# Order and grain of the first steps of a ternary feed-forward stage: rows in four groups, the second matrix's size read later, its ternary form made in three parts

## The reference

```python
def absmax_quant(x):
    gamma = jnp.max(jnp.abs(x), axis=-1, keepdims=True)
    x_hat = jnp.clip(x * Q_B / gamma, -Q_B + EPS, Q_B - EPS)
    return x_hat * gamma / Q_B
def ternarize_weights(w):
    gamma = jnp.mean(jnp.abs(w))
    return jnp.sign(jnp.round(w / (gamma + EPS))) * gamma
def bitlinear(x, w):
    xn = layer_norm(x)
    x_hat = absmax_quant(xn)              # value of the straight-through form
    w_hat = ternarize_weights(w)
    return jnp.einsum('bsd,od->bso', x_hat, w_hat)
h = bitlinear(x, w_fc)                    # 256 -> 1024
h = jax.nn.gelu(h, approximate=False)
return bitlinear(h, w_proj)               # 1024 -> 256
```

## Time and profile before

| what | value |
|---|---|
| time, median of 3 runs (lowest to highest) | 1629.67 us (1628.12 to 1630.09) |
| time of the profiled execution | 1631.58 us |
| its span, first to last instruction | 1629.8 us |
| mean granted TensorE clock | 0.964 |
| busy over the span: PE, DVE, ACT, POOL | 89%, 80%, 63%, 71% |
| the ternary feed-forward stage | 268.8 to 337.5 us |
| busy in that stage: PE, DVE, ACT, POOL | 45.99, 59.32, 41.80, 7.34 us of 68.70 |
| the rest of the kernel behind it | 337.5 to 1629.8 us |

### The profile page before, as it was taken

The page is one execution under the profiler, slowest core; times in us unless marked ns, Lnnn a source line. Parts: engine busy times, 40 slices in busy tenths (PEclk is TensorE's granted clock), DMA queues, the critical chain, the costliest instruction groups (busy, mean ns, idle before and its releaser), DMA issues. The chain is left out here.

```text
span 1629.8 us, 25527 instructions
## 1 busy us (share of the span) xinstructions
PE 1450.6 (89%) x8080; PEld 845.0 (52%) x8189; DVE 1297.1 (80%) x2596; ACT 1023.0 (63%) x2407; POOL 1153.8 (71%) x1064
## 2 busy tenths in 40 slices
PE   6697797757778999899999999989989999999988
PEld 4576464533544555455455455545545555554455
DVE  6876577879579889888978888888888888888865
ACT  2563563744366777666677666676766767767552
POOL 5673471112558889988878998878999888887742
PEclk9799898979899999999999999999999999999999
DMA  3000920020100001000000100000000000000020
GB/s 103 1 2 10 323 90 33 1 74 1 33 1 14 14 1 41 14 1 1 1 1 1 28 14 1 1 1 1 14 28 1 1 1 1 1 1 1 1 59 27
DMA packets 30974, 38.45 MB, mean 24 GB/s; under 512 B 4980, under 2 KB 26488, under 8 KB 30840
## 3 DMA queue, kind: packets, MB, share of 16 engines
q1 hardware_dynamic: 30840, 36.82, 7.1%
HBM read 35.76 MB, written 1.05 MB: 23 GB/s over the span
## 5 line engine op out<-in xcount | busy, mean ns | idle before, releaser
L2196 POOL TENSOR_TENSOR stream_acc<-stream_acc,stream_weights 128x512 f32<-128x512 f32 (+1 forms) x374 | 491.7, 1315 | 74.3 <-ACT stream_weights L2095 52.6
L2026 PE MATMUL stream_banks<-stream_weights,stream_v 128*128 128x512 f32 (+1 forms) x876 | 449.8, 597 | 0.1
L2089 ACT COPY stream_weights<-stream_banks 128x512 f32<-128x512 f32 (+1 forms) x438 | 255.8, 584 | 226.9 <-PE stream_banks L2001 215.8
L2268 DVE TENSOR_TENSOR stream_most<-stream_most,stream_banks 128x512 bf16<-128x512 bf16 (+1 forms) x416 | 284.2, 683 | 138.4 <-ACT stream_weights L2089 123.7
L2095 ACT ACTIVATE stream_weights<-stream_weights 128x512 f32<-128x512 f32 (+1 forms) x438 | 278.0, 635 | 66.6 <-DVE stream_weights L2254 62.7
L2254 DVE TENSOR_TENSOR stream_weights<-stream_weights,stream_banks 128x512 f32<-128x512 f32 (+1 forms) x438 | 296.4, 679 | 1.9 <-PE stream_banks L2016 0.6
L2203 POOL TENSOR_TENSOR stream_by_cos<-stream_by_cos,stream_by_sin 128x256 f32<-128x256 f32 x192 | 135.9, 728 | 78.7 <-DVE stream_by_sin L2314 78.7
L2001 PE MATMUL stream_banks<-stream_q_t_lo,stream_k_t_hi 128*128 128x512 bf16 (+1 forms) x477 | 181.4, 380 | 4.7 <-DVE stream_most L2268 0.9
L2001 PE MATMUL stream_banks<-stream_q_t_hi,stream_k_t_lo 128*128 128x512 bf16 (+1 forms) x479 | 182.2, 380 | 0.2
L2001 PE MATMUL stream_banks<-stream_q_t_hi,stream_k_t_hi 128*128 128x512 bf16 (+1 forms) x405 | 154.4, 381 | 26.7 <-DVE stream_most L2268 14.1
L2026 PEld LDWEIGHTS stream_banks<-stream_weights,stream_v 128*128 128x128 f32 (+1 forms) x876 | 145.0, 191 | 29.8 <-issue 4.3
(11 more groups left out here) (457 smaller groups left out, 3094.3 us busy)
## 6 DMA issues: line engine op xcount, KB each, us to landing
memory_raw_t<-in_ctx_t SPq DMA_DIRECT2D x4, 1601.0 KB, 9.4
memory_raw<-in_ctx SPq DMA_DIRECT2D x4, 1536.0 KB
row_ctx_t<-in_ctx_t SPq DMA_DIRECT2D x6, 512.0 KB, 3.6
early_raw<-in_L_xattn_Wq SPq DMA_DIRECT2D x4, 512.0 KB, 3.8
early_raw<-in_L_xattn_Wo SPq DMA_DIRECT2D x4, 512.0 KB, 3.9
row_ctx_t<-in_ctx_t SPq DMA_DIRECT2D x1, 1601.0 KB, 6.9
moe_raw_up<-in_L_ffn_wi SPq DMA_DIRECT2D x6, 256.0 KB, 4.9
model_x<-in_x SPq DMA_DIRECT2D x1, 1024.0 KB, 5.3
```

Of the source, the lines that this page charges most:

```text
L2026: nc.tensor.matmul(ps[:, 2 + n, :], v[0:r, g % 2, t, :], room(step)[0:r], start=(t == 0), stop=(t == KT - 1)).then_inc(weighed, 1)
L2089: nc.scalar.copy(room(step)[0:r], ps[0:r, step % 2, :]).then_inc(copied, 1)
L2196: nc.gpsimd.tensor_tensor(acc[0:r, h % 2, :], acc[0:r, h % 2, :], room(step)[0:r], ALU.add).then_inc(acc_ready, 1)
L2268: nc.vector.tensor_tensor(most[0:r], most[0:r], ps[0:r, step % 2, :], ALU.max).then_inc(maxed, 1)
```

## The change

The rows are prepared in four groups of two tiles (one batch row each). DVE goes through them in a new order: `measure_rows` (norm, largest value) and `scale_rows` (the rest), with `lower_rows(0)` between the two of batch row 1 and `lower_rows(1)` between the two of batch row 2. `turn_rows(b)` waits for its own group. The Abs of L1123 moves behind `high_rows(1)` on ACT. The multiplication by ones moves behind `up(0)` on PE and writes bank 7 in place of bank 2; the wait for `size_taken` moves from in front of `up(1)` to in front of `turn_rows(3)`, which writes bank 7. On DVE, reading the size and making the ternary matrix moves behind `quantise(0)`, in three parts: part 0 (the size and `below`) right behind it, part 1 behind `vary(0)`, part 2 behind `quantise(1)`.

```diff
-                for s in range(2):
-                    tiles = range(HALF_TILES * s, HALF_TILES * (s + 1))
-                    some = slice(tiles.start, tiles.stop)
-                    for t in tiles:
+                def measure_rows(b):
+                    some = slice(QT * b, QT * (b + 1))
+                    for t in range(QT * b, QT * (b + 1)):
                         last = nc.vector.tensor_scalar(rows[:, t, :], x[:, t, :], mean_var[:, t, 0:1], rs[:, 1, t:t + 1],
                                                        ALU.subtract, ALU.mult)
                     link(last)
                     link(nc.vector.tensor_reduce(top[:, 0, some], rows[:, some, :], AX_X, ALU.max, apply_absolute_value=True))
+
+                def scale_rows(b):
+                    some = slice(QT * b, QT * (b + 1))
                     nc.vector.tensor_scalar(up_size[:, some], top[:, 0, some], const["fc_mean"][:, 0:1], 1.0 / 128.0, ALU.mult, ALU.mult)
-                    if s == 1:
-                        lower_rows(0)
-                        lower_rows(1)
                     link(nc.vector.reciprocal(top[:, 1, some], top[:, 0, some]))
                     link(nc.vector.tensor_scalar(top[:, 1, some], top[:, 1, some], 128.0, None, ALU.mult))
-                    for t in tiles:
+                    for t in range(QT * b, QT * (b + 1)):
                         last = nc.vector.tensor_scalar(rows[:, t, :], rows[:, t, :], top[:, 1, t:t + 1], CLIP, ALU.mult, ALU.min)
                     link(last)
                     nc.vector.tensor_scalar(rows[:, some, :], rows[:, some, :], -CLIP, None, ALU.max).then_inc(rows_ready, 1)
...
+                def ternary(part):
+                    if part == 0:
+                        ve.wait_ge(size_spread, 1)
+                        nc.vector.tensor_scalar(mean_size[:], ps[:, 7, 0:1], 1.0 / (FF * DM), None, ALU.mult).then_inc(size_taken, 1)
+                        ve.wait_ge(size_taken, 1)
+                        link(nc.vector.tensor_scalar(per_size[:], mean_size[:], 1e-6, None, ALU.add))
+                        link(nc.vector.reciprocal(per_size[:], per_size[:]))
+                        nc.vector.tensor_scalar(mean_size[:], mean_size[:], 1.0 / 128.0, None, ALU.mult).then_inc(sizes_known, 1)
+                        ve.wait_ge(sizes_known, 1)
+                        nc.vector.tensor_scalar(below[:], raw[:], per_size[:, 0:1], -0.5, ALU.mult, ALU.is_lt)
+                    elif part == 1:
+                        link(nc.vector.tensor_scalar(flat, raw[:], per_size[:, 0:1], 0.5, ALU.mult, ALU.is_gt))
+                    else:
+                        nc.vector.tensor_tensor(flat, flat, below[:], ALU.subtract).then_inc(proj_ready, 1)
+
+                measure_rows(0)
+                scale_rows(0)
+                measure_rows(1)
+                lower_rows(0)
+                scale_rows(1)
+                measure_rows(2)
+                lower_rows(1)
+                scale_rows(2)
+                measure_rows(3)
+                scale_rows(3)
...
                 quantise(0)
+                ternary(0)
                 lower_rows(2)
                 lower_rows(3)
                 vary(0)
+                ternary(1)
                 for t in range(TILES):
                     if t + 1 < TILES:
                         quantise(t + 1)
+                    if t == 0:
+                        ternary(2)
                     h_rest(t)
...
-                ac.wait_ge(loaded, 16)
-                nc.scalar.activation(sized[:], raw[:], ACT.Abs, accum_out=size[:]).then_inc(sizes_ready, 1)
...
                 high_rows(0)
                 high_rows(1)
+                ac.wait_ge(loaded, 16)
+                nc.scalar.activation(sized[:], raw[:], ACT.Abs, accum_out=size[:]).then_inc(sizes_ready, 1)
                 gelu(0)
...
                 def turn_rows(b):
-                    pe.wait_ge(rows_ready, b // QT + 1)
+                    pe.wait_ge(rows_ready, b + 1)
+                    if b == 3:
+                        pe.wait_ge(size_taken, 1)
...
                 turn_rows(0)
                 turn_rows(1)
+                up(0)
                 pe.wait_ge(sizes_ready, 1)
-                nc.tensor.matmul(ps[:, 2, 0:1], ones[:], size[:], start=True, stop=True).then_inc(size_spread, 1)
-                up(0)
-                pe.wait_ge(size_taken, 1)
+                nc.tensor.matmul(ps[:, 7, 0:1], ones[:], size[:], start=True, stop=True).then_inc(size_spread, 1)
                 up(1)
```

More of the change, by code:

```diff
@@ L964, in ternary_ffn @@
         CLIP = 128.0 - 1e-6
-        HALF_TILES = TILES // 2
         raw = sb("raw_proj", [P, FC * DM])
@@ L1062, in _ @@
                     nc.vector.tensor_scalar(rows[:, some, :], rows[:, some, :], -CLIP, None, ALU.max).then_inc(rows_ready, 1)
[L1064 to L1068, removed]
@@ L1069, in _ @@
-                nc.vector.tensor_scalar(mean_size[:], mean_size[:], 1.0 / 128.0, None, ALU.mult).then_inc(sizes_known, 1)
-                ve.wait_ge(sizes_known, 1)
-                flat = tern[1][:].rearrange("p c n -> p (c n)")
-                nc.vector.tensor_scalar(below[:], raw[:], per_size[:, 0:1], -0.5, ALU.mult, ALU.is_lt)
-                link(nc.vector.tensor_scalar(flat, raw[:], per_size[:, 0:1], 0.5, ALU.mult, ALU.is_gt))
-                nc.vector.tensor_tensor(flat, flat, below[:], ALU.subtract).then_inc(proj_ready, 1)
+                flat = tern[1][:].rearrange("p c n -> p (c n)")
```

## The result

The changed kernel takes 1636.09 us (median of 6 runs, 1634.91 to 1637.29), the kernel before 1630.31 us on the same chip (also 6 runs). The medians differ by 5.8 us; the ratio is 1.0033, 95% interval [1.0021, 1.0044], which is 5.4 us more (3.4 to 7.2). Timed once more, ten runs gave 1.0030 [1.0020, 1.0040]. It is slower, as forecast. The predicted 1634.0 us lies 2.1 us under the first median; that median is just inside the prediction's wide range (it ended at 1636.2) and 0.4 us above the narrower one of its own case (1635.7).

A forecast was written before the change was run, and what follows sets the result against it. The change lies in one stage of 68.7 us, whose tiles run at DVE's pace. +4.3 us at `h_rest(0)` and 0 behind it take the median from 1629.67 to 1634.0 us, range 1631.2 to 1636.2.

The forecast's parts named there:

- the narrower one of its own case: Range of the main forecast alone, with bounds of groups, transposes and clock and 1 us of scatter: 1632.3 to 1635.7 us.
- What sets the end: Tiles behind `h_rest(2)` run at DVE's pace, busy 22.98 of 23.90 us, so a shift of `h_rest(0)` carries to the end.
- Four groups: Row preparation on DVE: each group of two tiles takes 3.01 us, adding 2.04 us of DVE work in all.
- The head: Start of the stage to `gelu(0)`: rows ready sooner, but the table load behind the Abs makes `gelu(0)` 0.19 us later.
- `quantise(0)`: On DVE, 3.57 us behind `gelu(0)` as before, at 286.50, after DVE idles 1.7 us.
- The new wait: `turn_rows(3)` on PE waits for bank 7, freed by L1065 behind `quantise(0)`: `square(0)` starts 4.32 us later, `h_rest(0)` at 299.91.
- Behind `h_rest(0)`: From `h_rest(0)` on, 0 further change, because `turn(1)` meets the same long PE idle time, some 4 to 5 us.
- The sum: Whole kernel: +4.3 us at `h_rest(0)` and 0 from there, median from 1629.67 to 1634.0 us, +0.26%.
- (1): Wait for bank 7 costs nothing; DVE's 4.55 us of inserted work decides alone: +2.8 us, 1632.5; chance 0.12.
- (2): PE's clock stays high through its idle time before `turn(1)`: +2.4 us, 1632.1; chance 0.10.
- (3): Not slower, DVE's idle times before `h_rest(0)` take up the ternary work: 1628.1 to 1630.0 us; chance 0.05.
- (4): Table load holds ACT 1.4 us more than its row, delaying everything behind `gelu(0)`: +5.7 us, 1635.4; chance 0.04.

The follow-up runs named there:

- the ternary work whole: Changed kernel with the size read and all three wide ternary instructions in front of `quantise(0)`: stage 68.84 us, ratio 0.9998 to the kernel before.
- the tiny Gelu: Changed kernel with a one-element Gelu behind `high_rows(0)` on ACT, loading the table early: stage 73.41 us, ratio 1.0015 to the kernel before.
- the improved version: Kernel before with 20 unread multiplications before `turn(1)`, `lower_rows(0)` earlier, last ternary instruction behind `quantise(1)`: 1628.17 us, ratio 0.9980.
- filler: Unread multiplications in PE's idle time before `turn(1)`: 23 in the changed kernel, ratio 1.0012; 20 in the kernel before, 0.9987; both against the kernel before.
- the size was read first: Changed kernel with the size read in front of `quantise(0)`, wide ternary instructions left where the change put them: stage 69.72 us, ratio 1.0004 to the kernel before.
- the late parts alone: Kernel before with size read and ternary parts behind `quantise(0)` and bank 7, but two groups and Abs first: stage 72.64 us, ratio 1.0021.
- the Abs first and filler: Changed kernel with the Abs back in front of `high_rows(0)` and unread multiplications before `turn(1)` on PE: stage 70.78 us, ratio 1.0019 to the kernel before.

## Why the prediction was right, point by point

- **What sets the end.** Right. DVE's stretch behind `h_rest(2)` carried each shift to the end: from `h_rest(2)` to the next stage 30.16 us before, 30.16 in the changed kernel, in both profiles of each. It does not hold for every variant: 31.00 with the ternary work whole, 30.49 with the tiny Gelu.
- **Four groups: 3.01 us each.** Right to 0.01, since the half-wide reduction had a row. The two new idle times were 0.60 and 0.54 (0.50 forecast).
- **The head.** PE turned the first rows 4.98 and the second 9.07 us into the stage (forecast 4.98 and 9.09). `gelu(0)` was held by the table load, 0.10 later than before (forecast 0.19). Right, and the load took 1.28 us with `gelu(0)` 0.01 behind it. So the drain that the Trainium skill ("ScalarE: Activation LUTs", What ACT_TABLE_LOAD costs) adds does not show here either; the measurement decides.
- **`quantise(0)`.** The step that was off: "`quantise(0)` follows 3.57 us behind `gelu(0)` as before, POOL's first mean included". It followed 2.96 us behind, since that mean took 0.38 us and not 0.98. I had taken its length as a property of the instruction; it was one of its neighbour on DVE (below). `quantise(0)` came 0.51 us sooner than before, not 0.19 later, and DVE's idle time in front of it was 0.85 us, not 1.7.
- **The new wait.** Right in place, releaser and clock: `turn_rows(3)` released by L1067. All behind it was 0.6 to 0.7 us sooner than forecast for the reason above: `square(0)` +3.62 (forecast +4.32), `h_rest(0)` +3.71 (+4.32).
- **Behind `h_rest(0)`.** I took 0; it was +0.29 in the first profile and -0.37 in the second, within the bounds given for the clock. That the two kernels meet the same clock there on average is not shown by two profiles of each.
- **The sum.** +4.3 forecast for the stage, +4.0 measured, +3.0 between the second profiles. The first is so close partly by luck: `h_rest(0)` moved by 0.6 us less than forecast, and 0.3 us of clock behind it made good half of that. The time moved by 5.4 and 4.9 us, which is 1 to 2 more than the stage. The forecast for the time rests on the stage alone, so that it fell short is this part, with no cause found. In both profiles of the changed kernel the stage also begins late (269.7, 269.4 against 268.8, 268.2 before), but so variable is this start (266.4 in the improved version) that I can't say whether that is the change or scatter. This stays open; the two ratios' intervals reach down to 1.0021 and 1.0020, 3.3 us, and with filler in both kernels the time moved by 3.4 us and the stage by 3.7.
- **The rivals.** (1), DVE's work decides alone, came true only when the size was read first: +1.3 us at `h_rest(0)`, not +2.8, because the size (0.76) then fell into DVE's idle time and `quantise(0)` was 0.6 earlier than I had it; 0.2 us more are not accounted for. (2), a high clock through the idle time before `turn(1)`, did not happen in the first profile. In the second `turn(1)` itself ran at the full clock, which fell behind it, and the stretch was 0.66 us shorter. Held by the filler the full clock was worth 2.2 us against the first profile and 1.6 against the second (at most 1.9 forecast). (3) and (4) did not occur.

## What to carry to other kernels

When a read that frees a buffer moves behind other work in one engine's order, look for everything queued behind the buffer's next writer on the other engines: here one 0.15 us read, put behind `quantise(0)`, held PE, ACT and again DVE, and doing it and its three small followers ahead of time won 2.45 us. Work can be moved into an idle time only as far as that idle time goes, counted at the place it is moved to: 4.55 us did not fit into 1.77, 1.28 us did fit into 1.48. Here a gap of PE in front of a chain on the critical path cost twice, by its length and by the low clock behind it, and multiplications that nobody reads bought the second part back (1.6 to 2.3 us of stage).

## What the runs showed of the hardware

POOL's first mean (L1019, one element in each of 128 partitions) took 0.98 us in the kernel before, 0.38 in the changed one and 0.24 with the late parts alone. The rows of DVE and of POOL at that time, first the kernel before:

```profile
283.72 1.28 DVE L1073 TENSOR_SCALAR ffn_tern_proj<-ffn_raw_proj,ffn_per_size 128x2048 f16<-128x2048 f32 x1
```

```profile
284.11 0.98 POOL L1019 TENSOR_SCALAR ffn_hmean<-ffn_hsum 128x1 f32<-128x1 f32 x1 [15.09 <-ACT ffn_h L1134]
```

the changed kernel:

```profile
284.77 0.61 DVE L1058 TENSOR_SCALAR ffn_rows<-ffn_rows,ffn_top 128x256 f32<-128x256 f32 x2
```

```profile
285.10 0.38 POOL L1018 TENSOR_SCALAR ffn_hmean<-ffn_hsum 128x1 f32<-128x1 f32 x1 [15.19 <-ACT ffn_h L1151]
```

the kernel before with the filler:

```profile
283.17 1.28 DVE L1073 TENSOR_SCALAR ffn_tern_proj<-ffn_raw_proj,ffn_per_size 128x2048 f16<-128x2048 f32 x1
```

```profile
283.21 1.34 POOL L1019 TENSOR_SCALAR ffn_hmean<-ffn_hsum 128x1 f32<-128x1 f32 x1 [14.72 <-ACT ffn_h L1134]
```

and the late parts alone, where DVE had no instruction at that time (idle from 280.05 to 283.60):

```profile
282.14 0.24 POOL L1019 TENSOR_SCALAR ffn_hmean<-ffn_hsum 128x1 f32<-128x1 f32 x1 [14.90 <-ACT ffn_h L1144]
```

In each of the first three POOL's instruction starts behind the start of the DVE instruction beside it and ends 0.09 to 0.10 us behind its end: 285.09 behind 285.00, 285.48 behind 285.38, 284.55 behind 284.45; so its length is set by how much of DVE's was left. In six further profiles it is the same within 0.02 us. With the tiny Gelu POOL's instruction began 0.06 us before DVE's L1059 and took 0.24 us; with the Abs first and filler it ran beside a reduction of DVE and took 0.24 us too. From these ends I conclude that it waits for the DVE instruction that started ahead of it. The Trainium skill ("SBUF — State Buffer", Who interferes with whom) says that DVE's tensor_scalar can enter modes that take a port pair shared with GpSimd, and that the other then blocks for the whole instruction; these rows agree. The price reaches ACT and DVE in the end: `centre(0)` waits for that mean. In the filler run of the kernel before, `gelu(0)` came 0.36 us sooner (the filler stands behind it in PE's order, so this is not its doing: over the first 3.90 us of `up(0)` the granted clock was 0.64, before 0.50), and `quantise(0)` at the same 17.48. POOL's mean stood until L1073 was through in both, but DVE itself came free from L1074 at 285.72, 0.01 us before `centre(0)` ended; the run does not tell which of the two held `quantise(0)`.

And the clock. Six profiles had 4.65 to 6.35 us of idle PE in front of `turn(1)`; in all six it began at the low level (1.94 us for its eight transposes), and the mean clock from `h_rest(0)` to `h_rest(2)` was 0.73 to 0.78 with 11.5 to 13.0 us of time. In the second profile of the changed kernel the gap was 3.63 us, `turn(1)` ran at the full clock (1.07 us for eight transposes, 1.94 in the first profile) and the clock fell behind it (mean 0.85). Where PE worked through or idled only 1.1 us before it, the clock was 1.00 and the time 10.0 us. So the same program can meet either course, and a difference of 1 us or so in a single profile of such a stage says nothing by itself.
